# Attention of a group ahead of the last query chunk, and the routing of older groups between VectorE's long operations

## The reference

```
q, k, v = split(x @ w_qkv); 16 heads of 8
q_proj = elu1(q @ proj); k_proj = elu1(k @ proj)          # 16 x 32 features
attn   = (q_proj @ (k_proj^T v)) / (q_proj @ sum(k_proj) + 1e-8)
x      = layernorm(x + attn @ w_out + b_out)
expert = argmax(x @ wr + br)                              # one of 8 per token
y      = gelu(x @ w1[e] + b1[e]) @ w2[e] + b2[e]          # only the token's expert is kept
out    = layernorm(x + y)
```

## Time and profile before

| | us |
|---|---|
| median of three runs | 236.87 |
| the profiled execution | 237.38 |
| its span, first to last instruction | 235.70 |

### The profile page before, as it was taken

One profiled execution on the slowest core, in us unless ns is written; L12 is line 12 of the kernel. 1 busy time (PEld: TensorE's weight loads), 2 busy tenths in 40 slices (PEclk: granted clock), 3 DMA queues, 4 the chain that ended last, 5 costly groups with the idle time before them and its releaser, 6 DMA issues.

```text
span 235.7 us, 5871 instructions
## 1 busy us (share of the span) xinstructions
PE 196.0 (83%) x1684; PEld 155.7 (66%) x1690; DVE 166.6 (71%) x539; ACT 141.5 (60%) x374; POOL 128.0 (54%) x161
## 2 busy tenths in 40 slices
PE   7989999999898887887865499899999999999000
PEld 2668888888554445444333189789989999999000
DVE  1577686867376899999998864777777766676600
ACT  3488887878476547647743527676666676666000
POOL 8338283646400108557557443463888766868860
PEclk9999999999999999999997758999999999999855
DMA  4799999999750001011011387551877787751100
GB/s 118 218 380 413 412 409 409 411 414 379 203 150 0 0 3 37 23 34 37 23 36 44 85 247 190 191 150 38 233 232 211 225 250 206 211 167 37 36 6 0
DMA packets 28416, 40.45 MB, mean 172 GB/s; under 512 B 3497, under 2 KB 18126, under 8 KB 28384
## 3 DMA queue, kind: packets, MB, share of 16 engines
q1 hardware_dynamic: 26112, 35.80, 46.9%
q0 software_dynamic: 2272, 4.27, 5.2%
HBM read 17.95 MB, written 22.56 MB: 172 GB/s over the span
## 4 chain that ended last, share of the span: by engine, by line
PE 50%; POOL 13%; issue 13%; DVE 10%; ACT 5%; DMA 4%; SPq 1%; DVEq 0%; ACTq 0%; POOLq 0%
PE pair L298 14%; PE pair L731 12%; PE pair L744 8%; POOL out_dram L506 5%; POOL sorted_rows L487 5%; PE bank L598 5%; PE bank L744 3%; POOL rstd L468 2%; DMA x_all<-sorted_rows 2%; PE pair L724 2%; PE pair L682 1%; POOL rstd L502 1%; DMA w_slot<-in_L_ffn_w_dram 1%; DMA wqkv_sb<-in_L_attn_w_qkv_dram 1%; PE bank L578 1%
## 5 line engine op out<-in xcount | busy, mean ns | idle before, releaser
L884 ACT ACTIVATE qfeat<-pair,w_sb 128x128 f32<-128x128 f32 x156 | 44.6, 368 | 27.8 <-PE pair L731 27.1
L731 PE MATMUL pair<-xsT,w_slot 128*128 128x128 f32 x312 | 43.5, 284 | 2.3 <-DMA w_slot<-in_L_ffn_w_dram 1.5
L487 POOL DMA_INDIRECT sorted_rows<-x,dest x32 | 31.9, 996 | 18.5 <-issue 11.6
L731 PEld LDWEIGHTS pair<-xsT,w_slot 128*128 128x128 f32 x312 | 39.6, 199 | 3.3 <-issue 2.6
L298 PE MATMUL pair<-wkv_part,xT_all 128*128 128x256 f32 x192 | 33.7, 320 | 2.0 <-ACT vals L811 0.8
L298 PEld LDWEIGHTS pair<-wkv_part,xT_all 128*128 128x128 f32 x192 | 28.4, 188 | 5.3 <-issue 5.3
L298 PE MATMUL pair<-xT_all,wq_part 128*128 128x512 f32 x96 | 31.7, 456 | 0.0
L744 PE MATMUL pair<-w_sb,qfeat 128*128 x232 | 31.6, 280 | 0.0
L838 ACT ACTIVATE qexp<-pair,minus_one 128x512 f32<-128x512 f32 x32 | 20.6, 678 | 15.5 <-PE pair L298 15.5
L515 POOL TENSOR_TENSOR ksum<-kfeat 128x512 f32<-128x512 f32 x12 | 16.2, 1350 | 25.0 <-DVE kfeat L954 25.0
L506 POOL DMA_INDIRECT out_dram<-x_all x26 | 26.0, 999 | 7.1 <-issue 5.8
(11 more groups left out here) (161 smaller groups left out, 362.3 us busy)
## 6 DMA issues: line engine op xcount, KB each, us to landing
sorted_rows<-pad_rows SPq DMA_DIRECT2D x11, 1584.0 KB, 23.1
w_slot<-in_L_ffn_w_dram SPq DMA_DIRECT2D x39, 256.0 KB
x_all<-in_L_attn_x_dram SPq DMA_DIRECT2D x8, 256.0 KB, 5.3
w_sb<-in_L_ffn_w_dram SPq DMA_DIRECT2D x4, 512.0 KB, 13.9
x_all<-sorted_rows SPq DMA_DIRECT2D x26, 66.0 KB, 2.6
xs<-sorted_rows SPq DMA_DIRECT2D x13, 66.0 KB, 2.8
w_sb<-in_L_ffn_b_dram SPq DMA_DIRECT2D x1, 512.0 KB, 7.6
sorted_rows<-x,dest POOLq DMA_INDIRECT x32, 2.4
```

The source lines that it names most:

```text
L487: g_.indirect_dma_start(out=sorted_rows, out_offset=bass.IndirectOffsetOnAxis(ap=dest[:, ring, i:i + 1], axis=0), in_=x1[:, ring, i, :], i ...
L731: last = mm(h_bank[t % 2][:, k * P:(k + 1) * P], w1_slot[:, t % WB, k * P:(k + 1) * P], xsT[:, t % 2, :], start=True, stop=True)
L884: a_.activation(hT[:, t % 2, k * P:(k + 1) * P], h_bank[t % 2][:, k * P:(k + 1) * P], ACT.Gelu, bias=w2_sb[:, bass.ds(w_at[t] + (FF + D + ...
```

## The change

What it does, in words:

- **Fourth query bank.** `QB` goes from 3 to 4; bank 7, which `ranks` used, becomes the fourth. `ranks` now writes into columns 384 on of bank 5 (groups 0 to 4, with a wait for `mid_ready` of the next group but one) and of bank 7 (groups 5 to 7).
- **TensorE, group step:** `attend(s-1)` stands ahead of `q_chunk(s, 3)`, `ranks` at the end. Twice 12 matmuls that nobody reads (`stay_awake`, 128 x 512 bf16) follow the loop: before `project(G-2)` and after `ranks(G-3)`.
- **VectorE, group step:** routing of a group is done one step later (s-3 instead of s-2), its rows too (s-4 instead of s-3), each short operation alone between two long ones of other groups. Functions are split for that, with the same operations. What the loop no longer reaches is written out by hand after it, the 30 table operations among it: those of the last tables now stand between the additions of tiles 4 to 8.
- **ScalarE:** `layer_norm(s-3)` instead of `(s-2)`, earlier in the step; the layer norms of groups 6 and 7 go to **GpSimd** (four `tensor_scalar` of 128 x 128 each).
- **GpSimd:** scatters of group s-4, three before and one after `rstd`; after the loop scatter 4, `rstd` 6, layer norm 6, two scatters of group 5, `rstd` 7, the other two, layer norm 7, scatters 6 and 7.
- **Expert tiles:** for tiles 0 to 9 the bias b2 is added by one more matmul on TensorE (one row of ones by the row of b2) and no longer by VectorE. `ranks(G-1)` moves behind tile step 3. Thirteen batches instead of twelve: five of 4 tiles, three of 3, five of 2 (before: eight of 4, three of 2, one of 1). GpSimd makes the next batch's `rstd3` between the two halves of each batch's stores. The wait for the last store is SP's.

```diff
-        QB = 3
+        QB = 4
...
+        def rank_slots(g):
+            return bank[5 if g < G - 3 else 7][:, 384:384 + (GT + 1) * E]
...
-        PARTS_AT = {2: (0, 1), 3: (2,), 4: (3,), 5: (4,)}
-        BATCHES = [range(i, i + 4) for i in range(0, 32, 4)] + [range(i, min(i + 2, NT)) for i in range(32, NT, 2)]
+        BATCHES = [range(i, i + 4) for i in range(0, 20, 4)] + [range(i, i + 3) for i in range(20, 29, 3)] + [range(i, i + 2) for i in range(29, NT, 2)]
         LAST_OF = {tiles[-1]: j for j, tiles in enumerate(BATCHES)}
-        NORMALISED_IN = {7: 0, 10: 1, 13: 2, 16: 3, 20: 4, 24: 5, 28: 6, 32: 7, 34: 8, 36: 9, 38: 10, 39: 11}
+        NORMALISED_IN = {7: 0, 10: 1, 13: 2, 16: 3, 20: 4, 23: 5, 26: 6, 29: 7, 31: 8, 33: 9, 35: 10, 37: 11, 39: 12}
+        BIASED_BY_DVE = range(10, NT)
...
+            sp.wait_ge(stored, 16 * NT)
...
+            def layer_norm(g):
+                par, ring = g % 2, g % XR
+                pool.wait_ge(shift_ready, g + 1)
+                pool.wait_ge(rstd_ready, g + 1)
+                for i in range(GT):
+                    last = g_.tensor_scalar(x1[:, ring, i, 0:D], res[:, par, i, :], rstd[:, par, i:i + 1], shift[:, par, i:i + 1],
+                                            ALU.mult, ALU.add)
+                last.then_inc(x1_ready, 1)
...
+                if 0 <= s - 4 < G:
+                    scatter(s - 4, range(0, 3))
                 if 0 <= s - 2 < G:
+                    inverse_deviation(s - 2)
                     token_numbers(s - 2)
-                    inverse_deviation(s - 2)
-                if 0 <= s - 3 < G:
-                    scatter(s - 3, range(GT))
+                if 0 <= s - 4 < G:
+                    scatter(s - 4, range(3, GT))
...
+            scatter(G - 4, range(GT))
             token_numbers(G - 2)
+            inverse_deviation(G - 2)
+            layer_norm(G - 2)
             scatter(G - 3, range(0, 2))
-            inverse_deviation(G - 2)
-            scatter(G - 3, range(2, GT))
             token_numbers(G - 1)
             inverse_deviation(G - 1)
+            scatter(G - 3, range(2, GT))
+            layer_norm(G - 1)
             scatter(G - 2, range(GT))
             scatter(G - 1, range(GT))
             inverse_deviations(0)
@@ -534,15 +556,10 @@
                 half = (len(tiles) + 1) // 2
                 for t in tiles[0:half]:
                     store(t)
-                if j + 1 < len(BATCHES) and len(tiles) == 4:
+                if j + 1 < len(BATCHES):
                     inverse_deviations(j + 1)
                 for t in tiles[half:]:
                     store(t)
-                if j + 2 < len(BATCHES) and len(tiles) < 4:
-                    inverse_deviations(j + 2)
-                if j + 2 < len(BATCHES) and len(tiles) == 4 and len(BATCHES[j + 1]) < 4:
-                    inverse_deviations(j + 2)
-            pool.wait_ge(stored, 16 * NT)
...
+            def stay_awake(n, out):
+                for _ in range(n):
+                    mm(out, ones_bf[:, :], share[:, :].to_broadcast([P, 512]), start=True, stop=True)
...
+                if g < G - 3:
+                    pe.wait_ge(mid_ready, g + 2)
...
-                if 0 <= s - 3 < G:
-                    ranks(s - 3)
-                if s < G:
                     q_chunk(s, 2)
                 if 0 <= s - 2 < G:
                     project(s - 2)
+                if 0 <= s - 1 < G:
+                    attend(s - 1)
                 if s < G:
                     q_chunk(s, 3)
-                if 0 <= s - 1 < G:
-                    attend(s - 1)
+                if 0 <= s - 3 < G:
+                    ranks(s - 3)
...
+                if t not in BIASED_BY_DVE:
+                    mm(y_bank[t % 4][:, 0:D], ones_row[:, :], w2_sb[0:1, bass.ds(w_at[t] + FF, D)], start=True, stop=False)
...
+            pe.wait_ge(q_done, C * (G - 1) + 1)
+            stay_awake(12, bank[0])
             project(G - 2)
             attend(G - 1)
             ranks(G - 3)
+            stay_awake(12, bank[2])
             turn(0)
             weights_of(0)
             up(0)
@@ -768,8 +795,9 @@
             ranks(G - 2)
             tile_step(1)
             tile_step(2)
+            tile_step(3)
             ranks(G - 1)
-            for s in range(3, NT):
+            for s in range(4, NT):
...
+                if 0 <= s - 3 < G:
+                    layer_norm(s - 3)
                 if s < G:
                     exp_q(s, 2)
+                if 0 <= s - 1 < G:
+                    inverse(s - 1)
                 if s < G:
                     exp_q(s, 3)
-                if 0 <= s - 1 < G:
-                    inverse(s - 1)
-                if 0 <= s - 2 < G:
-                    layer_norm(s - 2)
...
+            layer_norm(G - 3)
             inverse(G - 1)
             a_.preload_act_table_set("gelu_and_others")
             keep_rows(0)
             gelu(0)
             keep_rows(1)
-            tile_step(0)
-            layer_norm(G - 2)
-            for s in range(1, 4):
-                tile_step(s)
-            layer_norm(G - 1)
-            for s in range(4, NT):
+            for s in range(NT):
...
+                attn, route, row = 0 <= s - 2 < G, 0 <= s - 3 < G, 0 <= s - 4 < G
+                if attn:
+                    newton_first(s - 2)
+                if route:
+                    shift_of(s - 3)
+                if row:
+                    row_numbers(s - 4)
+                if attn:
+                    newton_second(s - 2)
+                if route:
+                    scale_scores(s - 3)
+                if row:
+                    next_rows(s - 4)
+                    pick_rows(s - 4)
+                if attn:
+                    normalise(s - 2)
+                if s:
+                    q_features(s - 1, 3)
+                if route:
+                    bias_scores(s - 3)
+                if row:
+                    rows(s - 4)
+                q_features(s, 0)
+                if route:
+                    best_score(s - 3)
+                q_features(s, 1)
+                if route:
+                    is_best(s - 3)
+                q_features(s, 2)
+                if route:
+                    count_best(s - 3)
+                if attn:
+                    add_x(s - 2)
+                    add_x_score(s - 2)
+                if route:
+                    choose(s - 3)
+                if attn:
+                    for i in range(GT):
+                        statistics(s - 2, i)
+                    for i in range(GT):
+                        moments(s - 2, i)
+                    add_epsilon(s - 2)
...
+            newton_first(6)
+            shift_of(5)
+            row_numbers(4)
+            newton_second(6)
+            scale_scores(5)
+            next_rows(4)
+            pick_rows(4)
+            normalise(6)
+            q_features(7, 3)
+            bias_scores(5)
+            rows(4)
+            used_rows(region)
+            best_score(5)
+            used_tiles()
+            is_best(5)
+            tiles_as_floats()
+            count_best(5)
...
+            add_x(6)
...
+            offsets_of(first)
+            assert done[0] == TAB_A
+            add_epsilon(6)
+            newton_first(7)
+            row_numbers(5)
+            newton_second(7)
+            next_rows(5)
+            pick_rows(5)
+            normalise(7)
+            rows(5)
+            shift_of(6)
+            scale_scores(6)
+            bias_scores(6)
+            best_score(6)
+            is_best(6)
+            count_best(6)
+            choose(6)
+            add_x(7)
+            add_x_score(7)
+            for i in range(GT):
+                statistics(7, i)
+            for i in range(GT):
+                moments(7, i)
+            add_epsilon(7)
...
+            add_row(0)
+            row_numbers(6)
+            row_statistics(0)
+            next_rows(6)
+            pick_rows(6)
+            row_moments(0)
+            rows(6)
+            add_row(1)
+            shift_of(7)
+            row_statistics(1)
+            scale_scores(7)
+            row_moments(1)
+            bias_scores(7)
+            add_row(2)
+            best_score(7)
+            row_statistics(2)
+            is_best(7)
+            row_moments(2)
+            count_best(7)
+            add_row(3)
+            choose(7)
+            row_statistics(3)
+            row_moments(3)
+            add_row_epsilon(3)
+            add_row(4)
+            row_numbers(7)
+            row_statistics(4)
+            next_rows(7)
+            pick_rows(7)
+            row_moments(4)
+            rows(7)
+            used_rows(region_up)
+            add_row(5)
+            used_tiles()
+            row_statistics(5)
+            tiles_as_floats()
+            row_moments(5)
+            tab().tensor_tensor(left[:, :], tiles_f[:, :], first_tiles[:, :], ALU.subtract).then_inc(tab_step, 1)
+            add_row(6)
```

(30 more changed lines are left out.)

245 lines of the change are left out of this document (114 added, 131 removed).

## The result

The changed kernel takes 234.95 us (median of four, 234.34 to 235.41); the kernel before took 236.71 (236.23 to 236.95) in the same session. The ratio is 0.9927, 95% interval 0.9898 to 0.9955. The forecast was 235.1, from 236.87. The profiled execution took 234.93 us with a span of 233.2, where the one of before took 237.38 with 235.7.

What follows compares the result with a forecast made beforehand. VectorE was taken to bound attention and TensorE the expert tiles. Terms -0.8 + 2.2 - 0.9 - 0.25 + 0.85 - 2.9 = -1.8 us took the median from 236.87 to 235.1, range 232.3 to 238.3.

Steps and rivals of the forecast that it cites:

- ten pairs: VectorE's attention step: ten dependent pairs pulled apart at 0.11 us each, 8.55 down to 7.45 us of work.
- the -0.8: Start of the expert tiles: first load at 130.5 instead of 131.33, `up(0)` at 134.2, 0.8 us earlier.
- Neither is worth more than the 8.1 of VectorE: Attention step: `attend` ahead of chunk 3 and the fourth bank gain nothing beyond VectorE's 8.1 us step.
- returns as late after `up(0)` as now: TensorE's clock at the start of the expert tiles: falls again and comes back as late as before, priced 0.
- Rival 2: TensorE's clock stays up from `up(0)` on, 3 us less, 232.1; chance 0.09.
- The bias product: TensorE, tiles 0 to 9: one-row bias matmul at 0.22 us each, +2.2 us, between 0 and 2.9.
- The load of tile 13: Expert tiles: later table operations delay the load to 164.0 to 164.4, so `turn(13)` waits, +0.85 us (0 to 1.6).
- Rival 1: Tables in time, no stall at tile 13, or a cheaper one-row product: 0.85 to 1.7 us less, 233.8; chance 0.16.
- rival 4: Table chain costs more, tile 13's load later; break-even at about 166.1; 237.4, slower or the same; chance 0.11.
- The tail: GpSimd's last stores end 6.8 us behind TensorE instead of 9.7: -2.9 us (-2.6 to -3.3).
- Rival 3: VectorE: short operations between long ones cost as in a chain, pairs save nothing, stall added; about 6 us later, 241; chance 0.07.
- rival 5: Gains and losses cancel: half of the tail's gain is lost to GpSimd's queue, 236.7; chance 0.15.

Runs made afterwards that it cites:

- all edits: Changed kernel with all tiles' bias on VectorE, last tables together behind `rows(7)`, `choose(7)` ahead of `add_row(3)`, `shift` behind `newton_second`: 226.61 us, ratio to before 0.9556.

## Why the prediction was right, and where it was not

- **Attention.** The mechanism holds: ten pairs, and a new stall before `shift` (0.57, predicted 0.6). A pair is worth 0.125 instead of 0.11, so the step is 7.87 instead of 8.13 and `newton_first(6)` 1.2 us earlier than forecast (my own numbers, 7.45 and 0.6, add up to 8.05, and I went on with 8.13). From there to the first load I had 11.1 us, measured 10.8. In it the first to the last of four scatters took 3.79, where I wrote 4.12 and added 3.9, and from the last one to the load 2.94, where I had 2.4 and an estimate of 0.65 that no row showed. That is the -0.8 that became -2.4: mostly a small error in a term that repeats.
- **"Neither is worth more than the 8.1 of VectorE"** passed over what the two edits prevent. With three banks the step is 8.40 and not VectorE's.
- **Blocks of matmuls and the clock.** "The clock falls again" was right; "returns as late after `up(0)` as now" was not, 4.3 us instead of 8.6. Low time behind `up(0)` was 2.8 (wait on GpSimd), 3.1 (`attend` last), 3.7 (tables together), 4.0 (three banks), 4.3 (changed kernel), 4.8 (old batches), 5.0 (no blocks), 8.6 (before), 8.7 (bias on VectorE), 8.8 (all edits), 9.1 (full rows), 10.2 (28 matmuls) and 12.2 us (`shift` later). The idle time ahead of `turn(0)` was 3.5 to 3.9 us in all but the kernel before (1.98) and the one with 28 matmuls (0.20), so it does not set this. What sets the return I can't say; these runs give no rule, and 1.7 us of the profiled gain go with it. Each of these times is of one execution, and executions of one kernel differ too: with `shift` later the four runs took 231.44 us at a mean clock of 0.962, and 234.69, 234.89 and 237.16 at 0.950, 0.949 and 0.941. So it is not shown that the change brought the earlier return. Rival 2 also took about 7 us of low time and 3 us for it, where the trace before has 8.6 behind `up(0)` and half of that is 4.3. The row of `project(6)` in the earlier trace rows shows the first four of its eight matmuls, 1.06 us; all eight take the 1.96 that I wrote, and with the blocks 1.19.
- **The bias product** is the term that failed: 0.22 from `down`, with the bound 2.9 for ten, against 6.1. My nearest row was a product over 128 rows, and the run with full rows shows that for such a product the price was right to 0.01. I took one row for at most as dear as 128, and no row of the trace spoke for that.
- **Layer norm 7 off ScalarE and `ranks(7)`**: -1.3 together, predicted -1.15; but the wait of `ranks(7)` did not shrink (0.74, predicted 0.65), and the waits for ScalarE gave nearly all of it. No run puts either of the two edits back by itself. On GpSimd each of the four operations of a layer norm takes 0.45 (I took 0.4), and the scatters behind it did not hold the load of tile 13, as assumed.
- **The load of tile 13**: predicted at 164.0 to 164.4, with 0.85 us of wait; measured 164.02 and 1.05. Rival 1 fell, and so did rival 4, which wanted the load at 166.1; the run with the tables together shows it from the other side.
- **The tail**: -2.9 (-2.6 to -3.3) against -2.57, 0.03 outside its bounds. The old batches put 2.55 back.
- **The end of the span**: 0 (-1.5 to +0.3) against -1.3, inside its bounds.
- **Rival 3** was refuted by the routing in a chain, rival 5 by the tail, rival 2 came true for half of the low time only.

## What to carry to other kernels

Count the pairs of dependent operations in a queue that has the bound: on VectorE a pair pulled apart gave 0.13 us, and it pays only while the new order puts no wait for another engine behind it, so place the operation that waits two long ones later. An edit that takes work off an idle engine and puts it on the one that bounds (the bias) is to be priced with that very shape, since the price taken from the nearest shape was off by a factor of three. Chains that release a load belong together and early, even if each gap looks free.

## What the runs showed of the hardware that I had not expected

- A product over one row costs TensorE 0.61 us between products over 128 rows, one over 128 rows 0.22, at the same width of 128.
- TensorE's clock came back between 2.8 and 12.2 us behind the same first product; in one run it fell while TensorE was busy. Work at 1.2 GHz takes twice as long as at 2.4 (from one block of eight matmuls of `attend` to the next 1.71 us in the run without the unread matmuls and 0.88 in the changed kernel), so half of the low time is its price, and by an estimate from these numbers, (12.2 - 2.8) / 2, two traces can differ by 4.7 us for it alone.
- The same final wait costs 1.3 us less of span on SP than on GpSimd (6.1 and 7.4 us from GpSimd's end to the span's).
